# A vision-transformer block on one core: the activations' low parts of single-expert blocks on VectorE instead of GpSimd, and one weight split half a block later

## The reference

```python
h = h + _L0_attn_ref(_layernorm(h, axis=-1), ...)
h = h + _L0_ffn_ref(_layernorm(h, axis=-1), ...)
# in _L0_ffn_ref: E = 8 experts of hidden width 192, shared width 768, top 2
dense_g = jnp.sum(jax.nn.one_hot(idx, n_exp, dtype=x.dtype) * gates[..., None], axis=-2)
g = jax.nn.silu(jnp.einsum('bsd,edh->bseh', x, w_gate))
u = jnp.einsum('bsd,edh->bseh', x, w_up)
expert_out = jnp.einsum('bseh,ehd->bsed', g * u, w_down)
routed = jnp.einsum('bse,bsed->bsd', dense_g, expert_out)
shared = jax.nn.silu(x @ ws_gate) * (x @ ws_up) @ ws_down
alpha = jax.nn.sigmoid(x @ sg_w + sg_b)
return alpha * shared + (1.0 - alpha) * routed
```

## Time and profile before

| what | us |
|---|---|
| median of 3 runs | 176.16 |
| lowest and highest | 175.26, 177.87 |
| the profiled execution, its own time | 175.75 |
| its span (first to last instruction) | 173.9 |
| VectorE busy, GpSimd busy | 120.5, 42.1 |
| feed-forward part, first matmul of block 6 | 120.08 |
| start of the last down product | 169.30 |

### The profile page before, as it was taken

How to read it: one execution, slowest core, us unless ns; L and a number is a source line. 1 busy time by engine, 2 the same in 40 slices (tenths; PEclk the granted TensorE clock), 3 DMA queues, 4 the chain that set the end, 5 groups by cost and what they waited for, 6 DMA issues and landing times.

```text
span 173.9 us, 4192 instructions
## 1 busy us (share of the span) xinstructions
PE 139.3 (80%) x1673; PEld 111.0 (64%) x1673; DVE 120.5 (69%) x297; ACT 91.0 (52%) x198; POOL 42.1 (24%) x55
## 2 busy tenths in 40 slices
PE   0449999903399988769806999999899999999992
PEld 0218777802177977659704567888777778878782
DVE  6299854699899996994626479787596562542753
ACT  0588865941277924444265769445645534343340
POOL 0000010000000000000000035536846858668430
PEclk9999999995579999999995589999999999999998
DMA  5999997000000000004991000048300000000003
GB/s 160 386 368 364 327 263 305 0 0 0 0 0 0 4 4 4 4 4 135 402 410 53 0 0 4 0 113 331 123 0 4 0 0 4 4 0 0 4 0 105
DMA packets 7391, 16.89 MB, mean 97 GB/s; under 512 B 800, under 2 KB 3612, under 8 KB 7372
## 3 DMA queue, kind: packets, MB, share of 16 engines
q1 hardware_dynamic: 7012, 16.29, 26.9%
q10 hardware_dynamic: 360, 0.34, 0.7%
HBM read 16.15 MB, written 0.47 MB: 96 GB/s over the span
## 4 chain that ended last, share of the span: by engine, by line
PE 50%; DVE 24%; ACT 9%; issue 5%; DMA 5%; ACTq 3%; POOL 2%; SPq 1%; DVEq 0%; POOLq 0%
PE PS L566 19%; PE PS L594 10%; PE PS L403 5%; DMA stage<-in_f_d_dram 5%; DVE piece L959 3%; DVE xsq L1115 3%; DVE mx L1111 2%; PE PS L322 2%; PE PS L415 2%; DVE vhl L1256 2%; PE PS L343 2%; PE PS L345 2%; PE PS L346 2%; PE PS L309 2%; POOL vhl L850 1%
## 5 line engine op out<-in xcount | busy, mean ns | idle before, releaser
L859 POOL TENSOR_TENSOR kq<-vhl,kq 128x296 f16<-128x296 f32 x35 | 29.5, 843 | 96.3 <-ACT kq L811 96.1
L1256 DVE SCALAR_TENSOR_TENSOR vhl<-PS,vhl 128x296 f32<-128x296 f32 x36 | 16.8, 466 | 21.6 <-POOL vhl L850 12.1
L804 ACT ACTIVATE vhl<-PS 128x296 f32<-128x296 f32 x36 | 15.0, 416 | 27.5 <-PE PS L566 27.5
L811 ACT ACTIVATE kq<-vhl 128x296 f16<-128x296 f32 x36 | 16.0, 445 | 5.5 <-DVE vhl L1256 5.5
L375 PE MATMUL PS<-cst,hn 128*128 128x128 f32 x10 | 4.0, 401 | 13.4 <-DVE hn L1035 13.4
L850 POOL TENSOR_TENSOR vhl<-vhl,xs 128x296 f32<-128x296 f32 x14 | 12.6, 903 | 5.5 <-issue 4.8
L1245 DVE TENSOR_TENSOR vhl<-vhl,xs 64x296 f32<-64x296 f32 (+1 forms) x18 | 10.2, 566 | 2.8 <-ACT vhl L804 2.6
L566 PE MATMUL PS<-XAh,piece 128*128 128x296 f16 x48 | 11.1, 316 | 0.2 <-DVE vhl L1256 0.2
L375 PEld LDWEIGHTS PS<-cst,hn 128*128 128x128 f32 x10 | 2.0, 201 | 14.0 <-DVE hn L1035 14.0
L566 PE MATMUL PS<-XAh,slab 128*128 128x296 f16 x48 | 10.0, 290 | 0.9 <-DVE vhl L1256 0.9
L343 PE MATMUL PS<-whl,xhl 128*128 128x193 f16 (+1 forms) x40 | 10.5, 262 | 0.0
(11 more groups left out here) (215 smaller groups left out, 403.0 us busy)
## 6 DMA issues: line engine op xcount, KB each, us to landing
slab<-in_w_inner_dram SPq DMA_DIRECT2D x3, 960.0 KB, 9.5
xs<-gate_rows_dram SPq DMA_DIRECT2D x8, 296.0 KB, 5.8
xs<-in_x_inner_dram SPq DMA_DIRECT2D x3, 592.0 KB, 10.5
stage<-in_f_a_dram SPq DMA_DIRECT2D x2, 768.0 KB, 10.4
stage<-in_f_b_dram SPq DMA_DIRECT2D x2, 768.0 KB, 11.7
stage<-in_f_d_dram SPq DMA_DIRECT2D x2, 576.0 KB, 13.2
xhl<-in_f_a_dram SPq DMA_DIRECT2D x1, 768.0 KB, 8.4
xhl<-in_f_b_dram SPq DMA_DIRECT2D x1, 768.0 KB, 9.3
```

The source lines that it names most:

```text
L804: A(silu[:, i % 2, :], PS[:, 3 + 2 * (i % 2), 0:HALF], ACT.Silu, scale=1.0 / XW).then_inc(S["a_silu"], 1)
L811: A(ah[:, f % ABUF, half * HALF:(half + 1) * HALF], hf[:, i % 3, :], ACT.Copy).then_inc(S["a_ah"], 1)
L859: G.tensor_tensor(al[:, f % ABUF, cols], hf[:, i % 3, :], ah[:, f % ABUF, cols], ALU.subtract).then_inc(S["g_al"], 1)
L1256: V.scalar_tensor_tensor(out=hf[:, i % 3, :], in0=PS[:, 4 + 2 * (i % 2), 0:HALF], scalar=SH / XW, in1=src[:, i % 2, :], op0=ALU.mult, op1= ...
```

## The change

The subtraction that gives a low part stays on GpSimd in the shared blocks and in blocks 7, 10, 13 and 16. In the eight blocks of one expert it goes to VectorE, behind the product of the next half; half 35 was there already. The waits follow: the counts of `g_al` and `v_al` are worked out by two new functions. The first low part of piece 2 is computed behind half 11 instead of half 10.

```diff
--- before.py
+++ after.py
@@ -77,6 +77,20 @@
 
 def two_experts(f):
     return f >= ST and (f - ST) % 3 == 1
+
+
+def low_on_pool(f):
+    return f < ST or two_experts(f)
+
+
+def pool_lows(i):
+
+    return sum(low_on_pool(k // 2) for k in range(i + 1))
+
+
+def dve_lows(i):
+
+    return i + 1 - pool_lows(i)
 
 
 def vit_kernel(nc, x_inner, x_ring, w_inner, w_ring, gb, consts, j_rev, ind, tok_b, cls, tab,
@@ -579,9 +593,10 @@
             def down(f):
 
                 pe.wait_ge(S["a_ah"], 2 * f + 2)
-                pe.wait_ge(S["g_al"], min(2 * f + 2, 2 * FT - 1))
-                if f == FT - 1:
-                    pe.wait_ge(S["v_al"], 1)
+                if low_on_pool(f):
+                    pe.wait_ge(S["g_al"], pool_lows(2 * f + 1))
+                else:
+                    pe.wait_ge(S["v_al"], dve_lows(2 * f + 1))
                 if f == 0:
                     pe.wait_ge(S["v_pad"], 2)
                 if f == ST:
@@ -862,7 +877,7 @@
             for i in range(2 * FT):
                 if 2 * ST <= i < 2 * FT - 2 and not two_experts(i // 2):
                     gated(i)
-                if i >= 1:
+                if i >= 1 and low_on_pool((i - 1) // 2):
                     act_low(i - 1)
 
 
@@ -1251,13 +1266,27 @@
                     dve.wait_ge(S["g_sg"], 4 * ((f - ST) // 3) + (f - ST) % 3 + half + 1)
                 if f >= ST:
                     src = sgate
-                if i >= 3:
-                    dve.wait_ge(S["g_al"], i - 2)
+                if i >= 3 and low_on_pool((i - 3) // 2):
+                    dve.wait_ge(S["g_al"], pool_lows(i - 3))
+                elif i >= 3:
+                    dve.wait_ge(S["v_al"], dve_lows(i - 3))
                 V.scalar_tensor_tensor(out=hf[:, i % 3, :], in0=PS[:, 4 + 2 * (i % 2), 0:HALF], scalar=SH / XW,
                                        in1=src[:, i % 2, :], op0=ALU.mult, op1=ALU.mult).then_inc(S["v_hf"], 1)
 
+            def act_low(i):
+
+                f, half = divmod(i, 2)
+                cols = slice(half * HALF, (half + 1) * HALF)
+                dve.wait_ge(S["a_ah"], i + 1)
+                if half == 0:
+                    dve.wait_ge(S["p_dn"], f - ABUF + 1)
+                V.tensor_tensor(al[:, f % ABUF, cols], hf[:, i % 3, :], ah[:, f % ABUF, cols],
+                                ALU.subtract).then_inc(S["v_al"], 1)
+
             for i in range(2 * FT):
                 product(i)
+                if i >= 1 and not low_on_pool((i - 1) // 2):
+                    act_low(i - 1)
                 if i == 0:
                     choose_first()
                 if i == 1:
@@ -1270,8 +1299,8 @@
                     gate_split()
                 if 5 <= i < 11:
                     ffn_low(1, i - 5)
-                if i in (10, 12, 13, 17, 18, 19):
-                    ffn_low(2, (10, 12, 13, 17, 18, 19).index(i))
+                if i in (11, 12, 13, 17, 18, 19):
+                    ffn_low(2, (11, 12, 13, 17, 18, 19).index(i))
                 if i == 2 * ST + 3:
 
                     dve.wait_ge(S["p_dn"], ST)
@@ -1280,9 +1309,7 @@
                                                scalar=small[:, 38, t:t + 1], in1=h2[:, t, :], op0=ALU.mult,
                                                op1=ALU.add).then_inc(S["v_acc"], 1)
 
-            dve.wait_ge(S["a_ah"], 2 * FT)
-            V.tensor_tensor(al[:, (FT - 1) % ABUF, HALF:N], hf[:, (2 * FT - 1) % 3, :],
-                            ah[:, (FT - 1) % ABUF, HALF:N], ALU.subtract).then_inc(S["v_al"], 1)
+            act_low(2 * FT - 1)
             for t in range(TILES):
                 dve.wait_ge(S["p_end"], t // 2 + 1)
                 V.scalar_tensor_tensor(out=fin[:, t, 0:D], in0=PS[:, t // 2, D * (t % 2):D * (t % 2) + D],
```

## The result

The changed kernel took 179.94 us (median of 6 runs, 177.74 to 179.99) against 175.95 us (6 runs, 175.13 to 177.87): ratio 1.018, 95% interval 1.0124 to 1.0236. The forecast was 178.3 us, a ratio of 1.012 to the 176.16 us it started from, within its range of 174.9 to 180.6. Two repeats of the same file gave ratios of 1.0128 (1.0074 to 1.0181) and 1.0115 (1.0027 to 1.0204).

The account below looks back on a forecast made before the run. TensorE was taken to bound the feed-forward stage, with 2.86 us of waits. Terms 0.78 + 0.11 + 0.73 + 0.35 + 0.35 = 2.32 us, added to 175.75 or 176.16, gave 178.3 us, range 174.9 to 180.6.

Parts of the forecast that it names:

- TensorE's waits as the measure: Feed-forward stage: TensorE alone is the chain, its waits total 2.86 us; the change adds 2.32 us.
- The signs named: Halves 17, 23 wait 0.8 us, 29, 35 0.4 to 0.6; second gate half 0.9 us; halves 16, 22, 28 wait less.
- Block 7: Product 14 comes 0.08 us earlier, product 15 at 130.22 for 129.44; later work shifts by 0.78 us.
- The pair: Odd half's 64-partition gate multiplications on VectorE: moved subtraction costs 0.39 us, GpSimd collision 0.48, so 0.87 us extra.
- Block 9: GpSimd's gating of half 19 ties with VectorE's moved subtraction; product 19 at 138.70 for 138.59, adding 0.11 us.
- Block 10: Product 20 at 141.13 for 141.27, product 21 at 143.34 for 142.61: 0.73 us more.
- Blocks 13 and 16: Even product 0.52 us earlier, odd product later; half 29 starts 0.35 us late, the same again in the second block.
- The split: Third piece's first split, moved behind half 11, lies before product 12, which waits for GpSimd anyway: zero.
- Rival A: No new collision: GpSimd's subtraction comes just behind both gate halves or waits for the pair; +0.4 us, chance 0.17.
- Rival B: Not slower: moved subtraction free after the even product, GpSimd's relief removes stalls; -1.4 us, chance 0.11.
- Rival C: More collisions: moved subtraction loses the tie with gating of halves 19, 25, 31, delaying products; +4.3 us, chance 0.08.
- Rival D: New stalls of up to 0.8 us bring a few us at half clock; +5.3 us, chance 0.04.

Follow-up runs that it names:

- the run in which GpSimd waits: Changed kernel, GpSimd's even-half subtraction in blocks 7, 10, 13, 16 also waiting until VectorE ended the odd half's gate pair: stage 49.54 us for 51.35, ratio 0.9973.
- four subtractions behind the pair: Kernel before, with only the subtractions of halves 13, 19, 25, 31 moved to VectorE, behind the next block's odd product: stage 48.59 us for 49.22, ratio 0.9997.
- the combined run: Kernel before with those four subtractions moved and third-piece splits behind halves 11, 11, 13, 17, 19, 21: stage 47.61 us, median 174.51 us, ratio 0.9885.

## Why the prediction was right, point by point

- **TensorE's waits as the measure.** Right. The stage grew by 2.13 us, the forecast was 2.32. Term by term, from the starts of TensorE's half blocks less the 2.07 us: block 7 gave 0.76 us for 0.78, block 9 0.08 for 0.11, block 10 0.66 for 0.73, blocks 13 and 16 0.31 and 0.32 for 0.35 each. The signs named came too: the second gate half takes 0.9 us, and halves 22 and 28 start without a stall.
- **Block 7.** With the 2.07 us by which everything starts later, product 14 was due at 130.08 and came at 130.09, product 15 at 132.29 and came at 132.26.
- **The pair.** The step on which the forecast hung. 0.87 us more was reckoned between the products, and 0.83 (2.17 - 1.34) came, within 0.01 in each of the four blocks; the 0.04 less is mostly that the first gate half was over 1.21 us after the even product's start, for 1.24 reckoned. GpSimd's subtraction ended 0.61 us after VectorE's first half, and the second half ended 0.32 us after GpSimd's subtraction: the two remainders that the prediction had read from the kernel before. So each wait lasted to the end of the other's instruction. The rule of the Trainium skill (SBUF — State Buffer, Who interferes with whom) that the two exclude each other for the whole instruction, by issue order, agrees: GpSimd's subtraction started at 155.97, the second half began at 156.17, behind it, and was held to 157.08.
- **Block 9.** The tie came as forecast, gating at 139.00, moved subtraction at 139.03 with 1.11 us. Product 19 at 140.73 for 140.77 due.

```profile
139.00 0.81 POOL L865 TENSOR_TENSOR vhl<-vhl,xs 128x296 f32<-128x296 f32 x1 [0.45 <-issue]
```
```profile
139.03 1.11 DVE L1283 TENSOR_TENSOR kq<-vhl,kq 128x296 f16<-128x296 f32 x1
```

- **Block 10.** Product 20 was due at 143.20 and came at 143.11, product 21 at 145.41 and came at 145.28. The splits took 0.74 us for the 0.77 assumed, and the pair 1.38.
- **Blocks 13 and 16.** Product 27 came at 157.12 where 157.28 was due.
- **The split.** Zero, as forecast; the run with it alone shows 49.20 us.
- **Rival A** (no new collision) falls with the pair's 1.38 us. What it priced, +0.4 us, is what the run in which GpSimd waits measures: 49.54 - 49.22 = 0.32.
- **Rival B** falls as well: VectorE had no idle time between the even product and the pair. Its 1.4 us of relief no run shows by itself: with four subtractions behind the pair 0.63 us came, after a new wait of down 6, and of the 1.61 us of the combined run 0.90 are the splits', which B didn't price.
- **Rival C** half happened: the subtraction lost the tie in blocks 9, 12 and 15, with 1.11 us each. But in 12 and 15 no half block of TensorE waited for it. Only in block 9 a split stands between it and the odd product; in block 12 product 25 still came 1.42 us after product 24 (151.22 to 152.64), and it was 1.47 in the kernel before. Product 25 was over at 153.09, and half 27, which needs it, follows half 26 (152.07) by its 1.26 us of work, without a gap:

```profile
153.33 0.41 PE L580 MATMUL PS<-XAh,xsq 128*128 128x296 f16 x2
```

- **Rival D** (the new stalls bring the clock down) didn't come: the granted clock was 1.00 in every window from 110 us to the end.

What was left out: that two executions of one program can differ by 2 us in the attention part. The three runs shown before (175.26, 176.16, 177.87) had one such run, and it was read as spread. The stage alone gives 2.13 / 175.95, a ratio of 1.012, and the two repeats came out at 1.0128 and 1.0115. Of the first six runs of the changed kernel four had the lower mean clock (0.914), the profiled one among them; most of the 1.6 us by which 179.94 lies above the forecast is that. No rival had it, since D tied a lower clock to the new stalls. That 179.94 still fell into the range is owed to the range's width and not to the reasoning; what the reasoning is borne out by is the stage.

## What to carry to other kernels

Before work is moved between VectorE and GpSimd, look not at their loads but at what will run on the other engine in the same tenths of a microsecond: in these traces a VectorE instruction with two operands in SBUF and a GpSimd one didn't overlap: whichever came second waited until the other's had ended (a product, with one operand in PSUM, took its usual 0.47 us at 123.00 in the kernel before beside a GpSimd subtraction from 122.87 that took its usual 0.75). A short instruction put ahead of a pair on the path cost 0.38 us for itself and 0.45 us because it shifted the pair into the other engine's work; behind the pair the stage was 0.32 us shorter than in the kernel before, in spite of a new wait of 0.6 us. And measure such a change by a stretch of the profile between two events of the bounding engine (here it repeated within 0.02 us), when whole runs scatter by 1% for reasons elsewhere.

## What the runs showed of the hardware

The granted clock of TensorE fell at different places in executions of the same program. In the changed kernel's first profile it was 0.50 from 82 to 86 us and 1.00 from 90 to 94, in its third 1.00 and 0.57 in the same windows:

```profile
82.00:86.00 4.00, 4.00 (x53) 3.57 (x50) 1.19 (x4) 0.60 (x4) 0.00 (x0) 0.50 1.00 373
...
90.00:94.00 4.00, 1.93 (x11) 1.40 (x9) 2.73 (x15) 3.22 (x7) 0.00 (x0) 1.00 0.78 311
```
```profile
82.00:86.00 4.00, 3.99 (x27) 3.67 (x27) 2.41 (x9) 1.20 (x8) 0.00 (x0) 1.00 1.03 406
...
90.00:94.00 4.00, 1.39 (x6) 1.29 (x7) 2.29 (x10) 2.45 (x7) 0.00 (x0) 0.57 0.44 174
```

In the first, TensorE was busy without a break as the clock stood at 0.50; in the third it fell behind a stretch in which TensorE hardly worked (0.36 us busy from 86 to 90 us). The three profiles with block 6 at 121.9 to 122.2 have a mean granted clock of 0.911 to 0.914 over the span, the ten others, with block 6 at 119.6 to 120.9, one of 0.937 to 0.949. As an estimate from these means and the spans, that is some 31 us at 1.2 GHz for 18 to 22: not only the place differs, but also the amount. For the changed kernel alone block 6 starts 2.3 to 2.5 us later with it. What decides between them stays open. Whether the change makes the lower clock likelier is open too: 10 of the changed kernel's 18 runs lay at 179.67 or above, all with a mean clock of 0.904 to 0.914, and 18 of 35 runs of the kernel before in the last batch at 177.46 or above, all with 0.900 to 0.922. The clock isn't the whole of the scatter either: the changed kernel's eight other runs, at 0.942 to 0.951, still spread from 177.12 to 178.97, which no run here explains.
